# 40 routed units are moved under the last batch's routing, and six batches of the shared network are moved to the end, in an attention and mixture-of-experts block on one core

## The chip, the cores and the metric

The program runs on one core of a Trainium2 chip. The metric is the device time of one execution, in microseconds (us). In the text PE is TensorE (matmuls), DVE is VectorE, ACT is ScalarE, POOL is GpSimd and SP is SyncE, which here only issues DMAs.

## The reference, cut to what matters

The input is 8 batches of 512 tokens with 128 channels. An attention layer with 16 heads runs first, with modulated layer norms around it. Then each token passes a shared network and two of eight routed experts:

```
x = x + ga * attention(norm(x) * (1 + ca) + sa)
h = norm(x) * (1 + cb) + sb
shared   = (silu(h @ shared_gate.T) * (h @ shared_up.T)) @ shared_down.T   # 128 -> 256 -> 128
scores, indices = top_k(sigmoid(h @ router_w.T + routing_bias), 2)         # 2 of 8 experts
w        = scores / sum(scores), spread over the experts
combined = sum over e of w[e] * (silu(h @ gate_w[e]) * (h @ up_w[e])) @ down_w[e]
out = x + gb * (shared + combined)
```

## The kernel before, in words

Every engine has its own program, written out in order; semaphores alone tie the engines together.

**Attention.** A loop over the 8 batches in 16 slots each. In the slots of batch b the kernel also finishes batch b-1: projection, second layer norm, router, ranks within each expert. For every (token, expert) pair a record of 130 floats (the normed token, its weight, the row that its result goes to) is scattered to DRAM (`routed`) by POOL, 8 indirect DMAs of 128 rows a batch (L690). Each expert has a region of its own in `routed`; `next_row` counts how far each region is filled. The scatters of batch b-2 go between POOL's work in the slots of batch b; those of the last two batches come after the loop.

**Shared network.** After the last batch's attention, `shared_up(b, j)` (PE, 4 matmuls of 512 columns, L1590) fills two PSUM banks, `shared_silu(b, j)` (ACT, L901) and `shared_act(b, j)` (DVE, L1162) make the product, `shared_dn(b)` (PE, 16 small matmuls, L1600) projects it back, and `shared_sum(b)` (DVE, L1170 and L1173) multiplies it with the gate `gb` and adds it to `x1`. All eight batches run here, and between them the last batch's projection, norm, router and ranks. When its counts are known, DVE makes tables (`region_tables`, `unit_tables`): which rows each unit reads and which expert it belongs to. SP then writes 128 rows of padding behind the last row of each of the eight regions (L594), one DMA an expert with its row read from a table first.

**Units.** The routed work is cut into 71 units of 128 records of one expert. For unit u SP loads the records (L604), at most 8 units ahead of the last unit that is finished (`yu_ready`); PE transposes them (`unit_T`, L1635); PE multiplies with gate and up (`unit_up`, L1646, 8 passes); ACT takes the silu (L927); DVE multiplies (`unit_act`, L1258); PE multiplies with down (`unit_dn`, L1655); ACT scales with the weight (`unit_y`, L932); POOL scatters the 128 results to DRAM (`send_unit`, L750). DVE also copies each unit's expert weights (L1270) and its result rows (L1253, which waits for the send of unit u-8). In step i PE runs `unit_up(i)`, `unit_T(i + 2)`, `unit_dn(i - 2)`, in that order, and the other engines likewise.

**End.** When all sends have landed, SP and ACT each load one result a batch and token (8 DMAs of 256 KB each, L445), and the sums, the gate and the addition to `x1` follow per batch: on DVE (L1306, L1313, L1316), for every second batch with the first sum on PE. SP and ACT store the output (L450).

Of the kernel before, what the change touches and what calls it, by code (L numbers as in the profile page):

```python
# [44 lines left out]
FAR = 1 << 20  # L45


def adaln_block(nc: bass.Bass, x, Wq, bq, Wk, bk, Wv, bv, Wp, bp, sh_gate, sh_up, sh_down,
                gate_w, up_w, down_w, router_w, routing_bias, c, wmod, out):
    ctx = ExitStack()  # L50
    with ctx:
# [104 lines left out]
        skip = sb("skip", [P, E])  # L156
        entered = sb("entered", [P, UNITS, E])
# [105 lines left out]
        table_chain = sem("table_chain")  # L263
        tables_ready = sem("tables_ready")
# [12 lines left out]
        sums_ready = sem("sums_ready")  # L277
# [76 lines left out]
        def sum_bank(b):  # L354

            return mx_bank[b // 2 % 2][:, 1, :]
# [81 lines left out]
        OUT_ORDER = (0, 2, 1, 4, 3, 6, 5, 7)  # L438

        def move_results(eng, half):  # L440
# [3 lines left out]
            for b in range(B):  # L444
                eng.dma_start(results[b][half], result_v[:, half, b]).then_inc(results_loaded[b], 16)  # L445
            for place, b in enumerate(OUT_ORDER):
                if place % 2 != half:
                    continue
                eng.wait_ge(out_ready, place + 1)
                eng.dma_start(out_v[:, b], x1[:, TT * b:TT * (b + 1), :]).then_inc(out_stored, 16)  # L450
# [5 lines left out]
        def _(sp):  # L456
# [134 lines left out]
            sp.wait_ge(tables_ready, 1)  # L591
            for e in range(E):
                row = sp.value_load(end_row[0:1, e:e + 1], min_val=e * REGION, max_val=e * REGION + TOKENS)
                sp.dma_start(routed_dram[bass.ds(row, P), :], pad_row[:]).then_inc(padding_written, 16)  # L594
            sp.wait_ge(padding_written, 16 * (E + 1))
            sp.wait_ge(scattered, BATCH_ROWS * B)
            sp.wait_ge(tables_ready, 3)
# [8 lines left out]
            for u in range(RING):  # L606
                load_unit(u, u, False)
            for it in range(1, UNITS // RING):
                for slot in range(min(RING, MOST_UNITS - RING * it)):
                    load_unit(RING * it + slot, slot, True)  # L610

            move_results(sp, 0)
# [6 lines left out]
        def _(pool):  # L619
# [87 lines left out]
            def scatter(b):  # L707
# [4 lines left out]
                rows_scattered(b)  # L712
# [30 lines left out]
            rstd(mv2, ve2, var2_ready, rstd2, rstd2_ready, stats2_ready, B_LAST)  # L743
            modulate2(B_LAST)
            scatter(B_LAST)
# [8 lines left out]
            for it in range(0, UNITS // RING):  # L754
                for slot in range(min(RING, MOST_UNITS - RING * it)):
                    send_unit(RING * it + slot, slot)
# [3 lines left out]
        def _(act):  # L760
# [149 lines left out]
            shared_silu(2, 0)  # L910
            shared_silu(2, 1)
            shared_silu(3, 0)
            evacuate_h2T(B_LAST, use(B_LAST, "h2T_last"))
            shared_silu(3, 1)
            exp_minus_logits(B_LAST, use(B_LAST, "lg_last"))
            for b in range(4, B):
                for j in range(IC):
                    shared_silu(b, j)
# [10 lines left out]
            def unit_y(u, slot):  # L929

                act.wait_ge(yu_full, u + 1)
                act.activation(y_u[slot], (pv_bank, misc)[slot % 2][:, 0:C], ACT.Copy, scale=w_u[slot]).then_inc(yu_ready, 1)  # L932

            def unit_step(i, k, turn, has_silu=True, has_xT=True, has_y=True):
                if has_silu:
                    unit_silu(i, k % RING)
                if has_xT:
                    unit_xT(i + 2, (k + 2) % RING)
                if has_y:
                    unit_y(i - 2, (k - 2) % RING)  # L940
# [15 lines left out]
        def _(dve):  # L956
# [207 lines left out]
            def shared_sum(b):  # L1164
# [3 lines left out]
                if b >= 1:  # L1168
                    dve.wait_ge(s_out, b)
# [545 lines left out]
```

## Time and profile before

| | us |
|---|---|
| median of 3 runs (lowest, highest) | 683.39 (681.89, 684.39) |
| the profiled execution, its span | 683.7 |
| attention, to the first matmul of the shared network | 0 to 483.4 |
| shared network, last batch's routing, tables, padding, first loads | 483.4 to 534.7 |
| 71 units, from the first `unit_act` to the last | 534.7 to 656.3 |
| last sends, result loads, final sums, stores | 656.3 to 683.7 |

The page gives one execution. An engine's busy time is the union of its instructions; "idle before" is the time in which it stood, with what ended it behind the arrow. PE's ends are modelled, so that one matmul's length is longer than the distance to the next start.

### The profile page before, as it was taken

The page shows a single profiled execution, that of the slowest core. Times are in us where ns is not written, and L with a number is a line of the kernel's source. Part 1 is how long each engine was busy: PE and PEld are TensorE (multiplying, and loading weights), DVE is VectorE, ACT ScalarE, POOL GpSimd, SP SyncE. Part 2 cuts the span into 40 slices and gives each one's busy share as a digit, 9 for nine tenths or more (in the row PEclk, how much of TensorE's full clock was granted, in tenths as well). Part 3 has the DMA queues.
Part 4 walks back from the last instruction along what each step waited for, and adds up shares of the span by engine and source line. Part 5 has one row for each costly group of instructions (what it writes and reads, how often), then busy time and mean ns, then how long its engine had stood idle before and what let it go on. Part 6 is the DMA issues. An engine that isn't in the chain of part 4 may idle for free.

```text
span 683.7 us, 11593 instructions
## 1 busy us (share of the span) xinstructions
PE 624.5 (91%) x3693; PEld 298.9 (44%) x3693; DVE 516.7 (76%) x1104; ACT 411.0 (60%) x846; POOL 264.0 (39%) x309
## 2 busy tenths in 40 slices
PE   4988999999999999999999999999998898888935
PEld 2332333233333333433333333232465888888931
DVE  5659888889988989888898888983368655555617
ACT  2145777777777687777777777778542445444520
POOL 4221022324352461452434233134434366566540
PEclk9669999999999999999999999999999999999987
DMA  3533132222321233223222231115102222222228
GB/s 101 146 56 97 52 101 76 66 82 72 94 86 62 75 97 95 79 78 105 72 70 75 70 98 52 39 40 173 53 0 70 64 74 78 69 78 79 70 68 320
DMA packets 50064, 56.92 MB, mean 83 GB/s; under 512 B 10281, under 2 KB 39243, under 8 KB 50004
## 3 DMA queue, kind: packets, MB, share of 16 engines
q1 hardware_dynamic: 42648, 43.11, 22.4%
q0 software_dynamic: 4320, 8.47, 3.6%
q10 hardware_dynamic: 3036, 4.61, 2.1%
q8 instruction: 30, 0.49, 0.3%
q14 instruction: 30, 0.25, 0.1%
HBM read 38.36 MB, written 17.92 MB: 82 GB/s over the span
## 4 chain that ended last, share of the span: by engine, by line
PE 68%; DVE 13%; ACT 6%; DMA 4%; issue 4%; SPq 2%; POOL 1%; another core or an unknown queue 0%; ACTq 0%; POOLq 0%; DVEq 0%
PE pv L1457 15%; PE st L1446 14%; PE mx L1431 13%; PE st L1646 9%; DVE neg_max L1012 6%; PE mx L1590 3%; ACT pt L803 2%; PE misc L1324 2%; PE misc L1351 2%; PE pv L1655 2%; PE misc L1655 2%; PE st L1600 1%; PE misc L1357 1%; DMA even_qk<-k_parts 1%; DVE ln L969 1%
## 5 line engine op out<-in xcount | busy, mean ns | idle before, releaser
L803 ACT ACTIVATE pt<-st 128x512 f32<-128x512 f32 x496 | 282.2, 598 | 106.0 <-PE st L1446 96.8
L1012 DVE TENSOR_REDUCE neg_max<-mx 128x2 f32<-128x1024 f32 x248 | 294.4, 1215 | 50.5 <-PE mx L1431 47.3
L1457 PE MATMUL pv<-pt,vs 128*32 128x512 f32 x1024 | 136.4, 605 | 0.3 <-ACT pt L803 0.3
L690 POOL DMA_INDIRECT routed<-rec,row_u x64 | 64.4, 1007 | 142.1 <-PE pv L1457 115.2
L750 POOL DMA_INDIRECT results<-qs,home_u x71 | 77.4, 1091 | 60.5 <-ACT qs L932 42.1
L1446 PE MATMUL st<-even_qk 74*128 74x512 bf16 x256 | 88.9, 388 | 4.1 <-DMA even_qk<-m_rows 2.2
L1446 PE MATMUL st<-qs,ks 74*128 74x512 bf16 x240 | 81.5, 383 | 1.8 <-ACT pt L803 1.1
L1431 PE MATMUL mx<-even_qk 72*128 72x512 bf16 x240 | 74.5, 392 | 6.0 <-DVE neg_max L1012 3.4
L1431 PE MATMUL mx<-ks,qs 72*128 72x512 bf16 x256 | 76.5, 380 | 2.8 <-DVE neg_max L1012 2.5
L1258 DVE TENSOR_TENSOR vs<-vs,st 128x256 f32<-128x256 f32 x71 | 29.7, 418 | 42.6 <-ACT vs L927 31.4
L1646 PE MATMUL st<-vs,pt 128*128 128x128 f32 x376 | 52.0, 282 | 10.3 <-DVE vs L1258 7.4
L398 POOL TENSOR_TENSOR qk_r<-qk_f,qk_parts 128x512 f32<-128x512 f32 x15 | 17.4, 1163 | 108.6 <-DVE qk_parts L390 108.4
L927 ACT ACTIVATE vs<-st 128x256 f32<-128x256 f32 x71 | 27.4, 386 | 45.7 <-PE st L1646 35.1
L1446 PEld LDWEIGHTS st<-even_qk 74*128 74x128 bf16 x256 | 20.7, 98 | 73.2 <-ACT pt L803 51.6
L1646 PEld LDWEIGHTS st<-vs,pt 128*128 128x128 f32 x376 | 46.8, 196 | 12.8 <-ACT vs L922 9.1
L1446 PEld LDWEIGHTS st<-qs,ks 74*128 74x128 bf16 x240 | 18.9, 98 | 67.5 <-ACT pt L803 51.6
L1457 PEld LDWEIGHTS pv<-pt,vs 128*32 128x32 f32 x1024 | 20.1, 108 | 52.9 <-issue 38.1
L1431 PEld LDWEIGHTS mx<-even_qk 72*128 72x128 bf16 x240 | 22.3, 100 | 37.9 <-DVE neg_max L1012 11.6
L1431 PEld LDWEIGHTS mx<-ks,qs 72*128 72x128 bf16 x256 | 23.8, 98 | 31.0 <-DVE neg_max L1012 7.8
L1270 DVE COPY pt<-even_qk 128x768 f32 x47 | 27.6, 588 | 6.2 <-issue 3.1
L1590 PE MATMUL mx<-h2T,shared_w 128*128 128x512 f32 x64 | 29.9, 600 | 1.9 <-issue 1.9
L1646 PE MATMUL st<-vs 128*128 128x128 f32 x192 | 25.9, 278 | 3.7 <-DVE vs L1258 2.5
(199 smaller groups left out, 792.7 us busy)
## 6 DMA issues: line engine op xcount, KB each, us to landing
ks<-routed SPq DMA_DIRECT2D x71, 65.0 KB
even_qk<-q_parts SPq DMA_DIRECT2D x48, 96.0 KB
qs<-q_parts SPq DMA_DIRECT2D x48, 96.0 KB
ks<-k_parts SPq DMA_DIRECT2D x48, 96.0 KB
even_qk<-k_parts SPq DMA_DIRECT2D x42, 96.0 KB
q_parts<-qk_parts SPq DMA_DIRECT2D x21, 128.0 KB
k_parts<-qk_parts SPq DMA_DIRECT2D x7, 384.0 KB, 2.3
x_in<-L_attn_x SPq DMA_DIRECT2D x8, 256.0 KB
```

The source lines that it names most:

```text
L690: pool.indirect_dma_start(out=routed_dram, out_offset=bass.IndirectOffsetOnAxis(ap=row_u[:, k, t:t + 1], axis=0), in_=rec[b.par][:, k, t, ...
L750: pool.indirect_dma_start(out=result_dram, out_offset=bass.IndirectOffsetOnAxis(ap=home_u[:, slot:slot + 1], axis=0), in_=y_u[slot], in_of ...
L803: act.activation(pt[n % 2][:, hh, :], score_bank(b, n, hh), ACT.Exp, scale=SCALE).then_inc(exp_done, 1)
L927: act.activation(silu_u[slot % 2], st_bank[slot % 2][:, 0:I], ACT.Silu).then_inc(silu_ready, 1)
L1012: dve.tensor_reduce(neg_max[g % 2][:, hh, 2 * half:2 * half + 2], mx_bank[half][:], AX_X, ALU.max, negate=True).then_inc(mx_free, 1)
L1258: dve.tensor_tensor(act_u[slot % ARING], silu_u[slot % 2], st_bank[slot % 2][:, I:2 * I], ALU.mult).then_inc(act_ready, 1)
L1270: dve.tensor_copy(w_unit[u % WRING], weights.rearrange("p e i -> p (e i)")[:, bass.ds(first, 3 * I)]).then_inc(w_ready, 1)
L1431: last = pe.matmul(mx_bank[half][:, t, :], qs[b.par][0:PROD, h, q0:q0 + P], ks[b.par][0:PROD, h, :], start=True, stop=True)
L1446: pe.matmul(score_bank(b, n, hh), ks[b.par][0:STACK, h, j * P:(j + 1) * P], qs[b.par][0:STACK, h, :], start=True, stop=True).then_inc(st_f ...
L1457: last = pe.matmul(pv_bank[32 * hh:32 * (hh + 1), :], vs[b.par][:, j, HG * g + hh, :], pt[n % 2][:, hh, :], start=(n % Y_SLOTS == 0), stop ...
L1590: last = pe.matmul(mx_bank[j][:, which, :], shared_w[:, IC * which + j, :], h2T[:, T * b:T * (b + 1)], start=True, stop=True)
L1646: last = pe.matmul(st_bank[slot % 2][:, m * P:(m + 1) * P], w_unit[u % WRING][:, m * P:(m + 1) * P], xuT[slot % 2], start=True, stop=True)
```

## The change

The units are cut into 40 early and 32 late ones. The early units hold only full blocks of 128 records from the first six batches, so they need neither the last two batches' records nor any padding. DVE makes their tables in slots 9 and 10 of the last batch (`early_regions`, `early_units`), and the units start after `shared_sum(0)`. The last batch's transposition, router, choice, ranks and scatters, and the tables of the late units, are interleaved with unit steps 0 to 24. SP writes the padding after the load of unit 31. The shared network of batches 2 to 7 runs after the last unit, and the final sum of a batch takes its result straight from PSUM: DVE adds the two results, adds the shared network's, multiplies with the gate and adds to `x1`. The sums on PE are gone. The order of batches in the end is changed, and SP alone stores the output.

The diff, cut:

```diff
+EARLY = 40
+LATE = UNITS - EARLY
+FIRST_SHARED = 2
+H2T_AT, LOGITS_AT, LIKELIEST_AT, CHOOSE_AT, RANK_AT, SCATTER_AT = 8, 10, 12, 14, 16, 16
+TABLES_AT = 18
...
-        OUT_ORDER = (0, 2, 1, 4, 3, 6, 5, 7)
+        OUT_ORDER = (2, 0, 3, 1, 4, 5, 6, 7)
...
+            sp.wait_ge(early_ready, 1)
+            sp.wait_ge(rows_free, 2 + B - 2)
+            sp.wait_ge(st_full, HG * SLOTS * B)
+            for u in range(MOST_UNITS):
+                if u == EARLY - RING:
+                    pad_regions()
+                if u == EARLY:
+                    sp.wait_ge(padding_written, 16 * (E + 1))
+                    sp.wait_ge(scattered, BATCH_ROWS * B)
+                    sp.wait_ge(tables_ready, 2)
+                load_unit(u, u % RING, u >= RING)
...
             modulate2(B_LAST)
-            scatter(B_LAST)
...
+            for u in range(MOST_UNITS):
+                if u == SCATTER_AT:
+                    hold(pool, rows_ready, B)
+                if SCATTER_AT <= u < SCATTER_AT + K_TOP * TT:
+                    scatter_rows(B_LAST, u - SCATTER_AT)
+                send_unit(u, u % RING)
...
+            for i in range(MOST_UNITS + 2):
+                if i < MOST_UNITS:
+                    unit_silu(i, i % RING)
+                if i + 2 < MOST_UNITS:
+                    unit_xT(i + 2, (i + 2) % RING)
+                if i >= 2:
+                    unit_y(i - 2, (i - 2) % RING)
+                if i == H2T_AT:
+                    evacuate_h2T(B_LAST, use(B_LAST, "h2T_last"))
+                if i == LOGITS_AT + 1:
+                    exp_minus_logits(B_LAST, use(B_LAST, "lg_last"))
+            for b in range(FIRST_SHARED, B):
+                for j in range(IC):
+                    shared_silu(b, j)
+                if b == FIRST_SHARED:
+                    load_results(act, 1)
...
+                    if n == 9 and last:
+                        early_regions()
+                    if n == 10 and last:
+                        early_units()
...
             shared_sum(0)
-            layer_norm2(B_LAST)
-            shared_act(2, 0)
...
+                if i == LIKELIEST_AT:
+                    likeliest(B_LAST)
+                if i == CHOOSE_AT:
+                    choose(B_LAST)
+                if i == RANK_AT:
+                    assign_rows(B_LAST, use(B_LAST, "rank_last"))
+                if i == TABLES_AT:
+                    late_regions()
+                if i == TABLES_AT + 2:
+                    late_entered()
+                if i == TABLES_AT + 4:
+                    late_rows()
+                if i == TABLES_AT + 6:
+                    unit_experts(EARLY, LATE, tables_ready)
...
+            def finish(b):
+                r = results[b][0]
+                add_results(b)
+                dve.wait_ge(s_down, b + 1)
+                dve.tensor_tensor(r, st_bank[b % 2][:].rearrange("p (t c) -> p t c", t=TT), r, ALU.add).then_inc(s_gated, 1)
+                dve.wait_ge(s_gated, b + 1)
+                gate_and_add(b)
...
+            shared_up(2, 0)
+            pe.wait_ge(yu_ready, MOST_UNITS)
+            shared_up(2, 1)
+            for b in range(FIRST_SHARED + 1, B):
+                shared_up(b, 0)
+                shared_dn(b - 1)
+                shared_up(b, 1)
             shared_dn(B - 1)
```

Three places show what the change does to the order on the engines. The first is SP at the load of unit 31 and the two loads behind it, in the changed kernel; `L594` and `L598` there are the load of a unit, `L604` and `L605` the padding.

```order
L594 TENSOR_LOAD unit_row
L594 ISA x2
L598 ISA
L598 DMA ks<-routed 128x130
L604 TENSOR_LOAD end_row
L604 ISA x2
L605 ISA
L605 DMA routed<-pad_row 128x130
L604 TENSOR_LOAD end_row
```

The group of the last five rows stands there eight times, and the load of unit 32 comes behind them; before, the eight stood ahead of the load of unit 0.

The second is DVE between the multiplications of units 11 and 14 of the changed kernel (`L1281` is `unit_act`, `L1276` the copy of the result rows, `L1293` the copy of the expert's weights, `L1060` to `L1065` is `likeliest`).

```order
L1281 TENSOR_TENSOR vs<-vs,st 128x256
L1276 CAST home_u<-ks 128x1
L1060 TENSOR_SCALAR probs<-probs 128x32
L1061 RECIPROCAL probs<-probs 128x32
L1063 MAX top_p<-probs 128x8 x4
L1065 MAX_INDEX top_e<-top_p,probs 128x8 x4
L1290 REGISTER_ALU x2
L1290 ISA
L1293 ISA
L1293 COPY pt<-even_qk 128x768
L1281 TENSOR_TENSOR vs<-vs,st 128x256
```

Before, `likeliest` stood directly ahead of `choose` and the shared products, and no unit was under way.

The third is ACT at the end. Before, it stood so (`L932` is `unit_y`, `L445` a result load, `L450` a store):

```order
L932 ACTIVATE qs<-pv,ks 128x128
L445 DMA qs<-results 128x512 x4
L445 DMA ks<-results 128x512 x4
L450 DMA out<-x 128x512 x4
```

In the changed kernel it stands so (`L913` is `shared_silu`, `L451` a result load):

```order
L935 ACTIVATE qs<-pv,ks 128x128
L913 ACTIVATE pt<-mx 128x512 x2
L451 DMA qs<-results 128x512 x4
L451 DMA ks<-results 128x512 x4
L913 ACTIVATE pt<-mx 128x512 x10
```

Ten of the twelve silus of the shared network now stand behind the eight result loads on ACT.

## Rows read from the trace of the kernel before

**Rows 1.** Busy us of PE, PEld, DVE, ACT, POOL; clock; DMA share, GB/s, by stage.

```profile
483.40:534.68 51.28, 48.09 (x244) 31.27 (x241) 35.53 (x100) 17.01 (x28) 21.93 (x23) 1.00 0.14 39
534.68:656.31 121.63, 107.86 (x905) 103.87 (x904) 69.62 (x208) 58.34 (x206) 73.09 (x67) 0.99 0.26 72
656.31:683.70 27.39, 10.41 (x24) 4.13 (x23) 13.71 (x21) 1.10 (x3) 4.34 (x5) 0.77 0.65 232
```

**Rows 2.** The chain of waits in the shared network: start, us, what.

```profile
490.85 1.72 PE mx L1590 x4
492.57 1.78 PE st L1600 x16
```

**Rows 3.** Timeline of DVE (start, us, engine, line), from the shared network to unit 0.

```profile
495.36 0.69 DVE L1170 TENSOR_TENSOR pt<-st,gb_bc 128x512 f32<-128x512 f32 x1 [1.43 <-PE st L1600]
...
529.86 1.03 DVE L1270 COPY vs<-even_qk 128x768 f32 x2 [0.59 <-issue]
...
534.68 0.41 DVE L1258 TENSOR_TENSOR vs<-vs,st 128x256 f32<-128x256 f32 x1
```

**Rows 4.** Timeline of PE, two unit steps in a row.

```profile
599.10 1.06 PE L1646 MATMUL st<-vs,pt 128*128 128x128 f32 x8
...
600.54 1.06 PE L1646 MATMUL st<-vs,pt 128*128 128x128 f32 x8
```

**Rows 5.** DVE in stretches: length, busy us and count, clock, DMA share, GB/s.

```profile
476.00:477.72 1.72, 1.56 (x14) 1.00 1.16 330
477.70:478.85 1.15, 0.98 (x7) 1.00 1.18 288
482.10:483.05 0.95, 0.84 (x5) 1.00 0.00 0
513.65:515.24 1.59, 1.41 (x8) 1.00 0.01 5
521.90:524.68 2.78, 2.64 (x7) 1.00 0.34 103
```

**Rows 6.** Timeline of DVE, late in the last batch.

```profile
471.81 0.36 DVE L1028 RECIPROCAL y_rden<-misc 128x32 f32<-128x32 f32 x1 [5.03 <-PE misc L1324]
```

**Rows 7.** Timeline of PE, the last batch's router.

```profile
505.07 0.96 PE L1393 MATMUL misc<-router_T,h2T_now 128*128 128x8 f32 x8
```

**Rows 8.** Timeline of ACT, behind the last batch's exponential.

```profile
506.54 1.28 ACT L901 ACT_TABLE_LOAD   x1
507.88 0.60 ACT L901 ACTIVATE pt<-mx 128x512 f32<-128x512 f32 x1
```

**Rows 9.** Timeline: padding writes, first two loads, first transposition, load 40 and its transposition.

```profile
514.87 10.68 SPq L594 DMA_DIRECT2D routed<-pad_row  x8
...
527.53 1.49 SPq L604 DMA_DIRECT2D ks<-routed  x2
...
529.62 0.30 PE L1635 MATMUL mx<-ident,ks 128*128 128x128 f32 x1
...
593.53 0.45 SPq L604 DMA_DIRECT2D ks<-routed  x1
...
598.54 0.27 PE L1635 MATMUL mx<-ident,ks 128*128 128x128 f32 x1
```

**Rows 10.** Timeline of PE, a unit's matmuls after a pause.

```profile
633.86 2.05 PE L1646 MATMUL st<-vs,pt 128*128 128x128 f32 x8 [2.69 <-DVE vs L1258]
```

**Rows 11.** The stretch after it, columns as in rows 1.

```profile
634.00:636.00 2.00, 2.00 (x10) 2.00 (x11) 1.20 (x4) 0.44 (x3) 1.15 (x2) 0.50 0.16 36
```

**Rows 12.** Timeline of the end: last send, ACT's later four loads, last DVE additions.

```profile
660.88 0.98 POOL L750 DMA_INDIRECT results<-qs,home_u  x1 [0.30 <-issue]
...
664.98 2.30 ACTq L445 DMA_DIRECT2D ks<-results  x4
...
679.26 0.69 DVE L1316 TENSOR_TENSOR x<-x,ks 128x512 f32<-128x512 f32 x1
...
680.58 0.69 DVE L1316 TENSOR_TENSOR x<-x,ks 128x512 f32<-128x512 f32 x1
```

More of the change, by code:

```diff
@@ new lines, in _ @@
+            for i in range(MOST_UNITS):
+                ahead = i + 2
+                if ahead < MOST_UNITS:
+                    if ahead == EARLY:
+                        dve.wait_ge(tables_ready, 3)
+                    if ahead % RING == 0:
+                        experts = [experts_of(ahead // RING)]
+                    unit_weights(ahead, ahead % RING, experts[0], ahead >= WRING)
+                unit_act(i, i % RING)
+                if ahead < MOST_UNITS:
+                    unit_rows(ahead, ahead % RING, ahead // RING, ahead >= RING)
+                if i == 0:
+                    layer_norm2(B_LAST)
+                if i == LOGITS_AT:
+                    add_router_bias(B_LAST, use(B_LAST, "lg_last"))
+                if i == LIKELIEST_AT:
[12 more added lines that the diff above has]
+                    unit_experts(EARLY, LATE, tables_ready)
@@ L1319, in _ @@
+            shared_act(3, 0)
+            finish(2)
+            shared_act(3, 1)
+            shared_act(4, 0)
+            finish_first(0)
+            finish(3)
+            shared_act(4, 1)
+            shared_act(5, 0)
+            finish_first(1)
+            finish(4)
+            shared_act(5, 1)
+            shared_act(6, 0)
+            finish(5)
+            shared_act(6, 1)
+            shared_act(7, 0)
+            finish(6)
+            shared_act(7, 1)
+            finish(7)
         @block.tensor
@@ L1680, in _ @@
-            for i in range(UNITS - RING, MOST_UNITS + 2):
-                unit_step(i, i - UNITS + RING, UNITS // RING - 1, has_up=i < MOST_UNITS, has_T=i + 2 < MOST_UNITS)
-            for b in range(1, B, 2):
-                pe.wait_ge(results_loaded[b], 16 * K_TOP)
-                if b >= 4:
-                    before = OUT_ORDER[:OUT_ORDER.index(b - 4) + 1]
-                    pe.wait_ge(out_chain, sum(2 - k % 2 for k in before))
-                for k in range(K_TOP):
-                    last = pe.matmul(sum_bank(b), ident[:], results[b][k].rearrange("p t c -> p (t c)"),
-                                     start=(k == 0), stop=(k == K_TOP - 1))
-                last.then_inc(sums_ready, 1)
+            shared_dn(1)
@@ new lines, in _ @@
+            pe.wait_ge(routed_loaded, 64)
+            for i in range(MOST_UNITS + 2):
+                if i < 2:
+                    pe.wait_ge(s_gated, FIRST_SHARED - 1 + i)
+                if i < MOST_UNITS:
+                    unit_up(i, i % RING, i >= 2)
+                if i + 2 < MOST_UNITS:
+                    unit_T(i + 2, (i + 2) % RING, (i + 2) // RING)
+                if i >= 2:
+                    unit_dn(i - 2, (i - 2) % RING, i >= 4)
+                if i == H2T_AT:
+                    h2_T(B_LAST, use(B_LAST, "h2T_last"))
+                if i == LOGITS_AT:
+                    router_logits(use(B_LAST, "lg_last"))
+                if i == RANK_AT:
+                    ranks(B_LAST, use(B_LAST, "rank_last"))
```

276 lines of the change are left out of this document (99 added, 177 removed).

## The prediction

> **What bounds the kernel now.** I first cut the span into stages and read each one's busy times. From 483.4 to 534.7 us PE is busy 48.1 of 51.3 us; in the units 107.9 of 121.6 us; in the end it is nearly idle, and the DMA engines are busy two thirds of 27.4 us [rows 1]. The reader is to see that PE, the bound of two stages, stands by in the third. I then read single steps there. A unit step takes PE 1.44 us [rows 4], but 71 units take 121.6, or 1.74 each: about a sixth goes into waits that come and go. A batch of the shared network costs PE two groups of 1.72 and one of 1.78 [rows 2], 5.2 us; six batches are 31.3 us. Moved into the end, they would seem to cost nothing. So I priced three things: how much earlier unit 0 starts, what the units lose by what is put between them, and how much longer the end becomes. All times below go against this execution's 683.7 us; the median of the runs shown is 683.4.
>
> **Earlier start.** After `shared_sum(0)`, whose first operation stands at 495.36 [rows 3] and which is two operations of some 0.7 us, DVE goes on at once with the units: 0.59 us for the table value and 1.03 for two copies of weights [rows 3] to 498.4, `shared_sum(1)` 1.4, two row copies 0.2, a third weight copy 0.5, so the first `unit_act` stands at 500.5 instead of 534.68 [rows 3]. PE is ready by then: its transpositions and `shared_dn(1)` end at about 497. The loads can't be late: SP issues them during the shared network's first two batches, and the experts' weights, in flight at 478.8, have landed at 482.1, when the DMA engines are idle [rows 5]. The early tables are some 21 small operations, 5.5 us at the 0.2 us of their like (1.59 for 8, rows 5 fourth) and a little more for the wide ones; DVE stands 5.03 us in that place [rows 6], so I count 0.5 lost. Without that cover they would cost up to 5.5 on PE's way to the last scores. Gain: 34.2 - 0.5 = 33.7; bounds 32 and 34.5.
>
> **What is put between the units.** PE gets the transposition, router and ranks; the router is 0.96 [rows 7], all three some 1.4 us, and PE is the bound, so 1.4 is the lower bound for the whole part. For the other engines I use what a step leaves over: DVE is busy 69.6 us for 71 units [rows 1], 0.98 each, and has register instructions between, so about 0.3 of a step is spare, and with two PSUM banks a product may come about 1 us late before it holds `unit_up` two units on. So a block alone costs its length less 1.0, and one that follows two steps later its length less 0.6:
> - `likeliest` 1.7 [rows 5]: 0.7. `choose` 1.15 [rows 5]: 0.2, its marks aren't urgent. `assign_rows` waits for the ranks, which PE makes behind `unit_dn`, about 1.3, and takes 0.95 [rows 5]: 1.2.
> - late tables: `late_regions` one operation more than the 1.59 [rows 5]: 0.8. `late_entered` 1.4: 0.8. `late_rows` is five operations of the row of 2.78 for seven [rows 5], over 32 units instead of 72, so 1.55: 0.9. `unit_experts` 0.7: 0.1.
> - layer norm and the wait for the router's sums: 0.9.
> - the exponential on ACT: two table loads and 0.23. A load is 1.28 and the next function starts 1.34 after it began [rows 8], so 2.9, and silu, `unit_xT` and `unit_y` stand behind it: 1.9.
>
> Together with PE's 1.4: 8.9. The upper bound is all lengths in full, 18. For the table load I weighed a page of the Trainium skill, "ScalarE: Activation LUTs", section "What ACT_TABLE_LOAD costs": each switch is 1.28 us and as much again for draining, 2.66 in all. By that, the sum would be 2.6 higher; the row shows the silu 0.06 us behind the load's end, so I keep the row.
>
> **The padding.** Before, SP's eight padding writes took 10.68 us from issue to issue [rows 9] while nothing waited but the first load. Now they stand between the loads of units 31 and 32, and all later loads are queued behind them. Two loads back to back take 1.49 us from the first issue to the end of the second, of 0.37 or so [rows 9], so a load costs SP 1.12 us, and a write has the same instructions. At that rate SP is 9.0 us busy with the eight, at their measured rate 10.7. Load 32 is thus 8.4 to 10.1 us later than in a row of loads 1.74 apart. What it has to spare is load 40's distance to its transposition, 598.54 - 593.53 = 5.0, less the shortest, 529.62 - 527.53 = 2.1 [rows 9]: 2.9. So PE stands 5.5 to 7.2 us at `unit_T(32)`, and with it `unit_dn(30)`. I take 5.5: POOL's eight scatters fall into the same time and hold the loads back a little anyway. A pause of this length brings the low clock: after one of 2.69 us eight passes took 2.05 instead of 1.06 [rows 4, 10], at a granted clock of 0.50 [rows 11]. I count 1.7 for it: the 0.99 of the eight passes and as much of the step's rest. Part: 7.2; bounds 3 (mostly hidden) and 9.
>
> **The end.** T is the last `unit_act`. The last send starts at T + 4.57, and ACT's loads end at 667.28, T + 11.0 [rows 12]. In the changed kernel ACT has done the two silus of batch 2 by then, but the other ten stand behind the loads, so DVE gets the product (3, 0) at T + 11.6. From there it has 10 products, six batches with four operations and two with three: 40 operations. Two of them, one waiting for the other, take 1.32 [rows 12], so 40 take 26.4. PE isn't done in time everywhere. Up to product (5, 1) DVE has first-batch results to fill in and waits once, 0.9, so that stands at T + 28.1. From then on a batch is a circle: `shared_dn` some 0.6 behind the product (it loads it as weights, an estimate), 1.78, `shared_up` 1.72, silu 0.8, product 0.65, that is 5.6, twice, then 2.6 for the last `shared_dn` and 2.0 for three operations: T + 44.0. The last store needs the 2.4 that it needs now (681.27 to 683.7). End T + 46.5 instead of T + 27.4: 19.1 longer. The result loads themselves are hidden by then. If ACT's queue didn't hold the silus, 2 us less; with PE at half clock for a part, more.
>
> **Sum.** 683.7 - 33.7 + 8.9 + 7.2 + 19.1 = 685.2. I forecast 685.2, no difference that counts: 0.5% (3.4 us) is about what a measurement of this kernel can tell.
>
> **Rivals.**
> - *The padding is hidden* (faster): if the eight writes leave load 32 within its 2.9 us, or if the late tables' steps stretch so that it has more to spare, 7.2 falls away, and half of the 8.9 goes into waits that are there anyway (the sixth of the stage in rows 1 against rows 4): 674 to 679. For it: single waits of 2 us stand in the units already [rows 10]. Against it: 9 us are three times what there is to spare. It decides at about 5 us less. Chance 0.28.
> - *POOL's scatters hold the units* (slower): one is 0.98 + 0.30 [rows 12], a pair of scatter and send 2.56 against a step of 1.74, so after eight units POOL is 6.5 behind. DVE's row copy of unit u waits for the send of u - 8, with some 4 us to spare. If this stall comes before the padding's and not in it, 2 to 4 more, and the upper half of the DVE bounds with it: 688 to 693. Chance 0.2.
> - *PE loses the clock in the end* (slower): in my schedule PE stands 1.8 and 2.2 us about T + 12 and T + 16 and is busy three quarters of the rest. At 1.2 GHz over some 10 us the end grows by 4.4, over all of it by 18: 690 to 703. Against it: in the units it is busy 89% at a clock of 0.99, waits included [rows 1]. "TensorE: Matmul & The Clock Gate" of the Trainium skill, section "A second HAM failure mode: psum-queue depth-cycling", says that PE can swing between its clocks when it idles briefly and often between groups; no row of these shows that. Chance 0.16.
> - The forecast, 680.0 to 686.8, keeps 0.36.
>
> **Range and chances.** 675 to 695 leaves out the best of the first rival and most of the clock's. Faster by over 0.5% 0.28, within 0.36, slower 0.36. The forecast's own range is 681 to 690, from the bounds of the padding and the end.
>
> **What would show it.** First `unit_act` at 500 to 501; units from there to the last in about 137.7 us (121.6 + 16.1); one stop of PE of over 4 us at unit 32, with SP's queue full of padding writes, and a clock of 0.50 behind it; ACT's eight loads ahead of its third silu in the end and DVE idle some 5 us there; the end 46 us long, DVE busy about 28 of them. The prediction is wrong if the stop isn't there, if the steps 8 to 24 aren't slower than the others, or if the end is shorter than 42.

## The result, and the profile after

The changed kernel takes 702.78 us (median of 4 runs, 693.68 to 703.91) where the kernel before took 682.64 on the same chip: ratio 1.025 (1.0185 to 1.032). The forecast was 685.2, the range ended at 695. It is slower, and outside the range. One of the four runs, at 693.68, lies inside it. The profiles below are read by their spans, which are about 1.7 us shorter than these times: 700.6 for the changed kernel, 683.7 before, from which the forecast was worked out.

The stages of the changed kernel, columns as in [rows 1]: last maxima to first shared product, to unit 0's `unit_act`, to that of unit 24, of 40, of 70, to the end.

```profile
469.69:495.07 25.38, 21.04 (x126) 5.74 (x124) 14.31 (x55) 18.20 (x36) 7.20 (x9) 0.93 0.45 133
495.07:513.90 18.83, 16.67 (x88) 12.12 (x84) 9.57 (x25) 5.85 (x11) 9.07 (x10) 0.91 0.22 55
513.90:565.05 51.15, 38.94 (x319) 36.48 (x318) 33.30 (x123) 24.04 (x76) 32.03 (x32) 0.98 0.22 61
565.05:602.03 36.98, 29.43 (x221) 28.73 (x220) 17.15 (x52) 13.67 (x47) 20.43 (x20) 0.89 0.31 82
602.03:653.50 51.47, 44.98 (x379) 43.12 (x379) 29.45 (x87) 25.70 (x90) 31.20 (x29) 1.00 0.25 69
653.50:700.60 47.10, 35.96 (x148) 21.51 (x148) 28.37 (x43) 7.91 (x15) 3.89 (x4) 0.92 0.38 134
```

In the kernel before, the same six stages took 20.75, 51.30, 40.90, 29.14, 51.59 and 27.39 us. The reader is to see that the units (139.6 us, forecast 137.7) and the end (47.1, forecast 46.5) are nearly as forecast, and that unit 0 is not: it starts at 513.90, forecast was 500.5 and 0.5 for the early tables. From 500.5 it is 13.4 us, which stand in three places.

**7.1 us lie ahead of everything that the change touches.** The last batch's last maxima stand at 469.69 instead of 462.62. One stretch of the setup, first of the kernel before, then of the changed one:

```profile
24.00:64.80 40.80, 35.21 (x119) 12.01 (x118) 26.50 (x36) 16.39 (x29) 7.58 (x11) 0.72 0.46 113
```

```profile
24.00:64.80 40.80, 33.66 (x86) 11.18 (x86) 21.74 (x31) 11.53 (x20) 7.84 (x11) 0.50 0.37 91
```

The granted clock is 0.50 throughout; in the kernel before it is 1.0 for good from 50.1 us. PE is nearly as busy (33.66 us and 35.21) and does 86 operations instead of 119. The instructions there are the same.

**4.6 us are the early tables** (25.38 against 20.75; I had counted 0.5). The timeline of DVE, some of the 21 operations:

```profile
473.95 0.17 DVE L1154 TENSOR_SCALAR padded_i<-padded 128x8 int32<-128x8 f32 x1
474.16 1.13 DVE L1121 TENSOR_SCALAR padded_i<-padded_i 128x8 int32<-128x8 int32 x1
475.32 1.19 DVE L1122 CAST padded<-padded_i 128x8 f32<-128x8 int32 x1
476.55 0.22 DVE L1123 TENSOR_TENSOR entered<-earlier,padded 128x64 f32<-128x64 f32 x1
...
477.98 1.19 DVE L1158 TENSOR_TENSOR taken<-taken,padded 128x8 f32<-128x8 f32 x1
...
482.66 0.35 DVE L1031 RECIPROCAL y_rden<-misc 128x32 f32<-128x32 f32 x1
```

What POOL did beside them:

```profile
472.63 1.27 POOL L686 TENSOR_TENSOR ln<-ln,mod_now 128x512 f32<-128x512 f32 x1 [1.79 <-POOLq L706]
473.98 2.51 POOL L691 TENSOR_TENSOR rec<-ln,mod_now 128x512 f32<-128x512 f32 x2
...
477.88 1.26 POOL L680 TENSOR_TENSOR x_ep<-x_ep,bp_ga 128x512 f32<-128x512 f32 x1
```

Three operations of eight elements a row take 1.1 to 1.2 us, six times the 0.17 of their like, and they end where POOL's 1.26 us products do (the last two at 476.5 and 479.1). The chain of 21 takes 9.0 us from 473.77, the reciprocal stands 12.97 us behind the maxima (9.19 before, [rows 6]), and PE waits for what follows it. The kernel before has the same products of POOL in the very stretch in which its DVE stood idle, 466.78 to 471.81:

```profile
466.66 2.51 POOL L681 TENSOR_TENSOR rec<-ln,mod_now 128x512 f32<-128x512 f32 x2
...
470.57 1.26 POOL L670 TENSOR_TENSOR x_ep<-x_ep,bp_ga 128x512 f32<-128x512 f32 x1
```

PE in the changed kernel, columns as in [rows 10], and the stretch behind its stop:

```profile
483.58 1.06 PE L1463 MATMUL misc<-router_T,h2T_now 128*128 128x8 f32 x8 [2.55 <-DVE y_tok L1034]
484.50 0.83 PE L1516 MATMUL mx<-qs,ks 74*128 74x512 bf16 x2
485.26 1.94 PE L1527 MATMUL pv<-pt,vs 128*32 128x512 f32 x8
...
488.57 1.07 PE L1527 MATMUL pv<-pt,vs 128*32 128x512 f32 x8
```

```profile
484.72:488.13 3.41, 3.41 (x13) 0.64 (x12) 1.94 (x17) 1.56 (x4) 0.00 (x0) 0.50 0.72 179
```

Behind the stop of 2.55 us the granted clock is 0.50 for 3.4 us, and the products take 1.94 instead of 1.07. **The remaining 1.7 us** are in the two shared batches (18.83 against a forecast of 17.1). They go with the chip: this stage takes 15.89 to 15.90 us in seven profiles on the faster chips of the experiments, and 18.8 to 19.2 in eight on the slower ones, this one among them.

The padding stop came where it was forecast, at unit 32: SP's queue, then PE. It is 4.0 us long (forecast 5.5; 4.75 and 4.90 in two later profiles).

```profile
570.73 9.11 SPq L605 DMA_DIRECT2D routed<-pad_row  x8
580.60 9.72 SPq L598 DMA_DIRECT2D ks<-routed  x8
```

```profile
582.64 0.33 PE L1689 MATMUL mx<-ident,ks 128*128 128x128 f32 x1 [4.03 <-DMA ks<-routed]
...
585.63 1.77 PE L1700 MATMUL st<-vs,pt 128*128 128x128 f32 x8
```

ACT's loads in the end came as forecast too: its third silu stands 6.44 us behind the second.

```profile
658.16 0.60 ACT L913 ACTIVATE pt<-mx 128x512 f32<-128x512 f32 x1 [1.12 <-issue]
661.25 1.80 ACTq L451 DMA_DIRECT2D qs<-results  x4
663.08 2.08 ACTq L451 DMA_DIRECT2D ks<-results  x4
665.20 1.08 ACT L913 ACTIVATE pt<-mx 128x512 f32<-128x512 f32 x2 [6.44 <-issue]
```

### The profile page after: what moved, and what is told of

It reads as the page before. It is cut to its first block, busy times and chain, and to the rows that moved or that the text cites. A ratio compares the mean times of both kernels' runs of the same rounds, so it can differ in the third digit from the quotient of the medians.

```text
span 700.6 us, 11557 instructions
## 1 busy us (share of the span) xinstructions
PE 631.8 (90%) x3677; PEld 302.4 (43%) x3677; DVE 524.0 (75%) x1126; ACT 412.0 (59%) x846; POOL 261.6 (37%) x309
## 4 chain that ended last, share of the span: by engine, by line
PE 63%; DVE 14%; issue 7%; ACT 6%; DMA 4%; SPq 2%; another core or an unknown queue 1%; POOL 1%; ACTq 1%; DVEq 0%; POOLq 0%
PE pv L1527 15%; PE st L1516 15%; PE mx L1501 14%; PE st L1700 5%; DVE neg_max L1015 5%; PE misc L1421 2%; PE misc L1394 2%; PE mx L1660 2%; PE st L1670 2%; ACT pt L815 2%; DMA even_qk<-k_parts 1%; PE pv L1709 1%; PE misc L1427 1%; DVE ln L972 1%
## 5 line engine op out<-in xcount | busy, mean ns | idle before, releaser
L1527 PE MATMUL pv<-pt,vs 128*32 128x512 f32 x1024 | 139.0, 615 | 0.3 <-ACT pt L815 0.3
L759 POOL DMA_INDIRECT results<-qs,home_u x71 | 73.9, 1041 | 52.6 <-ACT qs L935 31.5
L1516 PE MATMUL st<-even_qk 74*128 74x512 bf16 x256 | 90.4, 394 | 3.1 <-DMA even_qk<-m_rows 1.2
L1501 PE MATMUL mx<-even_qk 72*128 72x512 bf16 x240 | 77.3, 405 | 8.9 <-DMA even_qk<-k_parts 6.0
L1281 DVE TENSOR_TENSOR vs<-vs,st 128x256 f32<-128x256 f32 x71 | 29.7, 418 | 46.9 <-ACT vs L930 29.7
L1293 DVE COPY pt<-even_qk 128x768 f32 x47 | 28.2, 600 | 6.3 <-issue 4.2
L913 ACT ACTIVATE pt<-mx 128x512 f32<-128x512 f32 x16 | 9.4, 597 | 38.2 <-PE mx L1660 23.4
```

Of the source, the lines that this page charges most:

```text
L759: pool.indirect_dma_start(out=result_dram, out_offset=bass.IndirectOffsetOnAxis(ap=home_u[:, slot:slot + 1], axis=0), in_=y_u[slot], in_of ...
L1281: dve.tensor_tensor(act_u[slot % ARING], silu_u[slot % 2], st_bank[slot % 2][:, I:2 * I], ALU.mult).then_inc(act_ready, 1)
L1293: dve.tensor_copy(w_unit[u % WRING], weights.rearrange("p e i -> p (e i)")[:, bass.ds(first, 3 * I)]).then_inc(w_ready, 1)
L1501: last = pe.matmul(mx_bank[half][:, t, :], qs[b.par][0:PROD, h, q0:q0 + P], ks[b.par][0:PROD, h, :], start=True, stop=True)
L1516: pe.matmul(score_bank(b, n, hh), ks[b.par][0:STACK, h, j * P:(j + 1) * P], qs[b.par][0:STACK, h, :], start=True, stop=True).then_inc(st_f ...
L1527: last = pe.matmul(pv_bank[32 * hh:32 * (hh + 1), :], vs[b.par][:, j, HG * g + hh, :], pt[n % 2][:, hh, :], start=(n % Y_SLOTS == 0), stop ...
```

## Experiments

The runs were made in four sets, on chips of two kinds: on some the kernel before takes 665 us, on others, as on the first, 683 to 688. Each run is compared with the kernel before on its own chip.

**1. Both kernels again** (nothing edited; 665.27 us before).

> The changed kernel once more, to see how its first 66 us vary. In the profile of the change the code up to 66 us is the same as before, yet DVE's operations there stand 7.0 us later from 59 us on, and the granted clock stayed at 0.5 from 23.9 to 64.9 us instead of returning at 39.8 and for good at 50.1. Theory A (the setup can go two ways in any execution, whatever stands later in the program): the runs fall into two groups some 7 to 10 us apart, 692 to 694 and 701 to 704, and the unchanged kernel has both groups too. Theory B (the change brings it, by where its code or data lie): nearly all runs stand at 701 to 704, and the unchanged kernel's stay at 681 to 684.

> The kernel before once more, beside it. Theory A: some of its runs stand 7 to 10 us above the others, at 689 to 692. Theory B: all of them stand at 681 to 685, and the clock in its profile returns for good near 50 us.

Measured: changed 677.11, ratio 1.0155 (1.0112 to 1.0199); before 665.36. The long stretch of low clock was there again, from 23.0 to 64.0 us, and the last maxima stood 3.4 us later than in the kernel before. Neither theory came out whole. Four of the changed kernel's six runs stand at 676.8 to 679.4 and two at 669.5 and 672.9, while all 35 of the kernel before stand between 661.6 and 672.7, without a second group: this speaks against A, and the two lower runs against B. The kernel was run once more, in the set of experiment 3:

> The changed kernel, nothing altered. Two of its two profiled executions had the lower clock from 23 to 64 us, four of four of the others had it only to 41 to 53 us. Theory (the setup, whose code the change doesn't touch, falls into the longer lower clock by chance in any kernel): its times split into two groups 3 to 4 us apart, and the profile may show either. Rival (this program falls into it nearly always): 677 us, 0.5 to 64 us in the profile again.

Measured: 673.18 (670.39 to 685.55), ratio 1.0133; this time the clock was back at 51.1 us, so the program doesn't fall into the long stretch every time. The stages of this profile, and behind them those of the kernel before on the chip of the first set:

```profile
462.97:488.28 25.31, 20.98 (x127) 5.69 (x125) 14.23 (x55) 18.09 (x36) 7.18 (x9) 0.93 0.45 133
488.28:504.17 15.89, 15.07 (x88) 10.54 (x84) 9.47 (x25) 5.96 (x11) 9.07 (x10) 1.00 0.26 64
504.17:547.63 43.46, 37.41 (x320) 36.04 (x320) 33.11 (x124) 25.24 (x76) 30.41 (x29) 1.00 0.25 70
547.63:579.36 31.73, 25.77 (x209) 25.26 (x208) 18.11 (x52) 14.31 (x47) 21.30 (x22) 0.89 0.33 93
579.36:622.73 43.37, 43.37 (x391) 43.37 (x391) 30.26 (x88) 27.39 (x89) 32.05 (x30) 1.00 0.29 83
622.73:668.64 45.91, 35.17 (x152) 20.58 (x151) 28.34 (x43) 8.16 (x15) 4.46 (x5) 0.96 0.38 139
```

```profile
465.32:486.08 20.76, 19.16 (x127) 5.66 (x125) 6.19 (x34) 18.00 (x36) 7.21 (x9) 1.00 0.54 159
486.08:536.98 50.90, 47.99 (x244) 31.28 (x241) 35.77 (x99) 16.90 (x28) 22.21 (x23) 1.00 0.14 40
536.98:571.18 34.20, 34.20 (x309) 34.20 (x308) 24.08 (x74) 21.37 (x71) 23.88 (x22) 1.00 0.30 84
571.18:594.49 23.31, 23.31 (x212) 23.31 (x210) 16.93 (x49) 14.85 (x49) 17.42 (x17) 1.00 0.33 92
594.49:637.58 43.09, 43.09 (x389) 43.09 (x388) 29.57 (x89) 27.14 (x88) 32.05 (x31) 1.00 0.31 85
637.58:664.66 27.08, 11.18 (x24) 4.32 (x23) 13.71 (x21) 1.10 (x3) 3.84 (x4) 0.79 0.65 235
```

Here the sum can be read without the setup: -35.0 + 4.6 (start), +9.3 (steps 0 to 24), +8.4 (24 to 40), +0.3, +18.8 (end) make +6.3 us (before rounding); forecast was +1.5. The first profile has the same differences stage by stage to 1 us, but for its 7.1 us in the setup and 2.5 in the shared batches.

**2. Each suspected cost mended alone** (the same set as 1). The early tables go into the slot of `choose`, behind the router's softmax:

```diff
-                    if n == 9 and last:
+                    if n == 14 and last:
                         early_regions()
-                    if n == 10 and last:
                         early_units()
```

> The changed kernel with the early tables made in slot 14 of the last batch, behind the choice, instead of in slots 9 and 10. In the change's profile the tables took DVE 8.8 us (473.8 to 482.7) where it had 5.0 free, the router's matmuls waited 2.55 us for it, the clock fell to 0.5 for 3.4 us, and the first shared matmul stood 4.6 us later against the last batch's slot 9. Theory (tables on PE's way): the first shared matmul comes 4 to 5 us earlier measured from slot 9, the time falls by 4 to 5 against the changed kernel. Rival (ACT's exponentials bound the last slots and take it back, or the tables now delay the ranks of batch 6 and with them POOL): less than 1.5 us.

Measured: 668.12, ratio 1.0037 (1.0005 to 1.0068), 9.0 less than unmended. Two of the long operations, now beside an idle POOL, in DVE's timeline:

```profile
482.11 0.17 DVE L1121 TENSOR_SCALAR padded_i<-padded_i 128x8 int32<-128x8 int32 x1
482.32 0.17 DVE L1122 CAST padded<-padded_i 128x8 f32<-128x8 int32 x1
```

All 21 now take 5.5 us. The last maxima to the first shared product take 20.75 us again: 4.6 of the 9.0. Another 3.1 is that this profile's setup had its clock back at 52.7 us; the rest is not assigned.

The padding goes out as one write ahead of each load of units 29 to 36:

```diff
-                if u == EARLY - RING:
-                    pad_regions()
+                if u == PAD_FROM:
+                    sp.wait_ge(tables_ready, 1)
+                if PAD_FROM <= u < PAD_FROM + E:
+                    pad_region(u - PAD_FROM)
```

> The changed kernel with one padding write ahead of each of the loads of units 29 to 36, instead of all eight ahead of the load of unit 32. In the change's profile PE stood 4.0 us for the transposition of unit 32, with the clock at 0.5 behind it. Theory (the eight writes in a row hold the loads longer than they have to spare): no stop of PE over 2 us at units 29 to 37, and 4 to 6 us less. Rival (SP is short of time over the whole stretch: 2.3 us a load against a step of 1.5 to 1.7): the stop is only spread, 0 to 2 us less.

Measured: 671.69, ratio 1.0100 (1.0075 to 1.0125). Steps 24 to 40 go from 31.5 to 27.3 us, 4.2 back of the 8.4; the stop at unit 32 is gone. The tables, still in slots 9 and 10, cost more here: low clock for 17 us goes with their stop, and the stage took 31.25 us.

```profile
474.57:491.63 17.06, 17.06 (x67) 4.12 (x67) 3.56 (x27) 7.40 (x15) 0.00 (x0) 0.50 0.25 64
```

**3. Both mended, the scatters spread, the setup kept busy** (665.1 us before).

> Both mendings in one kernel: the early tables in slot 14, and one padding write ahead of each load of units 29 to 36. Theory (two separate costs of the change, 9.0 us for the early tables in slots 9 and 10 and 4.2 us for the padding's eight writes in a row): the two add, so some 664 us where the kernel before takes 665.3 and the unchanged changed kernel 677.1, ratio 0.998; last maxima to first shared product 20.75 us, steps 24 to 40 in 27.3 us. Rival (the tables' gain was mostly a good state of the setup, which came by chance): the ratio stays at 1.004 or above, near that of the tables alone, whatever the padding gives.

Measured: 663.97, ratio 0.998 (0.9957 to 1.0004). The rival as it was put (1.004 or more) is out, and the two costs add, but not as 9.0 and 4.2. Beside the unmended kernel of its own set (673.18) the gain is 9.2 us, and the stages hold 4.6 for the tables and 4.6 for the padding; the 9.0 of experiment 2 had some 3 us of the setup's chance in it, as the rival suspected. Steps 24 to 40 take 27.2 us, still 3.9 more than before. POOL's queue has no pause from 530.85 to 569.00 us:

```profile
530.85:569.00 38.15, 32.43 (x280) 31.46 (x279) 26.20 (x88) 19.88 (x66) 29.61 (x29) 1.00 0.37 101
```

These are 29 transfers, most of them 1.28 us apart (busy 0.96 to 1.4, then 0.30 of issue), and DVE waits 7.7 us in five waits of units 0 to 40 for result sends to land (5.6 of them in steps 24 to 40); in the unmended kernel it was 9.6 in six, in the kernel before none. PE waits for no load there. So I spread the scatters:

```diff
-                if SCATTER_AT <= u < SCATTER_AT + K_TOP * TT:
-                    scatter_rows(B_LAST, u - SCATTER_AT)
+                if SCATTER_AT <= u < SCATTER_AT + 2 * K_TOP * TT and (u - SCATTER_AT) % 2 == 0:
+                    scatter_rows(B_LAST, (u - SCATTER_AT) // 2)
```

> The kernel of both mendings, with the last batch's eight scatters on GpSimd's queue ahead of every second send (units 16, 18 ... 30) instead of ahead of eight sends in a row (16 to 23). In the run with the padding spread, steps 24 to 40 still took 27.3 us, 4.0 more than in the kernel before, and VectorE waited there 2.94, 0.94 and 1.22 us for the result sends. Theory (GpSimd at 1.28 us an indirect transfer falls behind in units 16 to 23, at two transfers for a unit of 1.45 us): these waits shrink to 1 us or less in all, steps 24 to 40 take 24 to 25 us, and the time falls by 2 to 4 us against the kernel of both mendings. Rival (the sends are late for another reason, or GpSimd, 40 of 55 us busy, only falls behind later): steps 24 to 40 stay at 27 us, or the wait moves to load 40, which needs the last scatter: 0 to 1 us gained.

Measured: 662.63, ratio 0.9969 (0.9943 to 0.9995); steps 24 to 40 still 27.1 us. The theory's waits shrank there (from 5.6 us, the longest 3.0, to 4.1, the longest 1.0), but the time of the stage did not: PE now waits 2.8 us in four waits for SP's loads, which stand between the padding writes (a load and a write 2.2 us together, a unit step 1.45). Shortening one wait brought up the next, much as the rival had it.

The setup gets four more products ahead of the wait for the first keys.

```diff
+                if fill == DIRECT_FILLS:
+                    for _ in range(4):
+                        pe.matmul(pv_bank[:], ident[:], direct[1][0][:], start=True, stop=True)
                 max_scores(*fill_of(fill))
```

> The changed kernel, with four more products of 128x128 by 128x512 in TensorE's queue at the place in the setup where it waits for the first keys (2.3 to 6.0 us idle); their result is never read. Theory (the setup's 3 to 7 us come from the lower clock behind that idle stretch): the clock is at 1.0 for good by 53 us or sooner, the last maxima come 3 us sooner than in the changed kernel, and the median is 3 us lower. Rival (the idle stretch has nothing to do with it, or the late keys set the times themselves): lower clock to 64 us and the same time, or up to 4 us more where the products stand in the way.

Measured: 675.85, ratio 1.0161, no gain. Its profile had the clock back for good at 51.1 us, but so had the unedited run beside it: this settles nothing. Its early tables were followed by 13.7 us of low clock, and that stage took 29.63 us.

**4. GpSimd's queue, the loads, the modulation.** The first three of these fell on a chip where the kernel before takes 687.12 us, without the kernel of both mendings beside them; so a second set (687.66 before) repeated two of them with it.

```diff
                     scatter_rows(B_LAST, u - SCATTER_AT)
+                    if u % 2 == 1:
+                        scatter_rows(B_LAST, u - SCATTER_AT, spare_dram)
```

> The kernel of both mendings, with four more indirect transfers on GpSimd's queue (behind the scatters of units 17, 19, 21 and 23; the same rows into a spare buffer that nobody reads). In the kernel of both mendings GpSimd runs without a pause from 531 to 569 us, at 1.28 us a transfer, while units 16 to 40 are worked on. Theory (with the padding spread, GpSimd's queue is what the units wait for there: 24 sends and 8 scatters at 1.28 us are 41 us, and 24 units alone would be 35): steps 24 to 40 take 27.2 + 4 x 1.28 = 32.3 us, and the time rises by 5 us to 669. Rival (GpSimd is busy but nobody waits for it; steps 24 to 40 are long for the padding writes that still stand between the loads): no more than 1 us.

> The kernel of both mendings again, as the yardstick for the three others of this set: the runs with more scatters, with the loads by SyncE and with the modulation on VectorE fell on a chip where units 0 to 70 take 20 us more in every kernel (the kernel before included) and no run of the kernel of both mendings stood beside them. Theory (the mendings leave the changed kernel level with the one before): ratio 0.995 to 1.002 where the kernel before takes 665 us, and some 1.005 where it takes 685.

> The four more indirect transfers on GpSimd's queue again, now beside the same kernel without them. Theory (GpSimd's queue is what units 24 to 40 wait for once the padding is spread): 5.1 us above the kernel of both mendings, all of it in steps 16 to 40. Rival: within 1 us of it.

Measured: 698.35 (first set); 692.93 with the mendings alone (ratio 1.0085, 1.0043 to 1.0127) and 698.92 with four more transfers (1.0172, 1.0122 to 1.0222): 6.0 us (give or take 4.5, an estimate from the two intervals) for 5.1 us of GpSimd's time. In the first set the next run below, whose units are those of both mendings, serves as the yardstick: 692.61, or 5.7 less. So more transfers cost time, and of the size expected. The mechanism isn't shown. In the profiles of the second set the stretch from unit 0 to 24 takes 62.6 instead of 55.2 us and 24 to 40 takes 32.4 instead of 30.6; in the first set it is 59.7 and 58.7, then 34.7 and 31.9. And the wait that the theory goes by, DVE for a result send, is 1.2 us in all in either kernel of the second set. The mended kernel itself is level with the one before at 665 us and 0.85% slower here.

All result loads by SyncE:

```diff
-            load_results(sp, 0)
+            load_results(sp)
...
-                if b == FIRST_SHARED:
-                    load_results(act, 1)
```

> The kernel of both mendings, with all sixteen loads of results issued by SyncE, none by ScalarE. The prediction's step: ScalarE's eight loads hold its queue behind the last unit, and the third batch's silus with it, for 1.8 us, with VectorE idle for some 5 us there. Theory (the step as predicted): the end, from the last unit_act, goes from 46.8 us to 45, and the time falls by 1 to 2 us to 662 or 663. Rival (the sixteen loads on one queue come later than the sums want them, or the end is bound by the results' sends): no gain, or up to 2 us lost.

Measured: 692.61, ratio 1.0088 (1.0056 to 1.012), against 1.0085 for the mendings alone in the other set: no gain to be seen in the time, though the end is 43.2 us in this profile and 44.4 in the other. In DVE's timeline the third product no longer waits for ACT's queue, and the first addition waits for its load instead:

```profile
653.83 0.69 DVE L1248 TENSOR_TENSOR pt<-pt,mx 128x512 f32<-128x512 f32 x1 [1.03 <-ACT pt L915]
657.03 0.69 DVE L1344 TENSOR_TENSOR qs<-qs 128x512 f32<-128x512 f32 x1 [2.51 <-DMA qs<-results]
```

The last batch's modulation on VectorE, at units 1 to 3:

```diff
+                if i == 1:
+                    dve.wait_ge(ln2_ready, TT * B)
+                    dve.tensor_tensor(ln2[:], ln2[:], mod_now[B_LAST.par][:, 2:3, :].to_broadcast([P, TT, C]),
+                                      ALU.mult).then_inc(h2_chain, 1)
+                if i in (2, 3):
...
+                    dve.tensor_tensor(rec[B_LAST.par][:, i - 2, :, 0:C], ln2[:],
+                                      mod_now[B_LAST.par][:, 1:2, :].to_broadcast([P, TT, C]), ALU.add).then_inc(h2_ready, 1)
```

> The kernel of both mendings, with the last batch's three modulation products (1.52, 1.51 and 1.51 us on GpSimd, at units 1 to 3) made by VectorE, ahead of its work for units 2 to 4. Theory (two engines that read and write the same memory hold each other up: VectorE's weight copies of 1.23 us at units 3 to 5, 0.55 elsewhere, and the small operations of 1.2 us in the early tables, are as long as they are because a GpSimd product runs beside them; and the first send waits behind these products): the copies take 0.56 us each, VectorE's wait of 2.0 us for the sends at unit 8 goes, VectorE pays 3 x 0.7 = 2.1 us, and steps 0 to 24 come out 1 to 3 us shorter, 40.5 to 42.5 us. Rival (the long copies have another cause, such as TensorE's or the transfers' use of the memory): the copies stay at 1.23 us and steps 0 to 24 grow by some 2 us.

> The last batch's modulation products on VectorE again, beside the same kernel with them on GpSimd. The first run showed every weight copy at 0.55 us (1.23 where GpSimd's products ran beside them) and steps 1 to 4 at 1.46 us (1.55). Theory: steps 0 to 24 are 1 to 3 us shorter and the time falls by as much. Rival (what is won at the copies is paid for by the products on VectorE, and the backlog of GpSimd at units 16 to 40 eats the earlier start): the same time within 1 us.

Measured: 690.79 (ratio 1.0053) and 691.92 (1.0063; 1.0 less than the mendings alone in its set, which is within the scatter). Weight copies in DVE's timeline, of the kernel of both mendings, then of this one:

```profile
505.76 0.56 DVE L1293 COPY pt<-even_qk 128x768 f32 x1
506.65 1.22 DVE L1293 COPY pt<-even_qk 128x768 f32 x1
508.18 1.23 DVE L1293 COPY pt<-even_qk 128x768 f32 x1
```

```profile
505.34 0.56 DVE L1296 COPY pt<-even_qk 128x768 f32 x1
506.80 0.56 DVE L1296 COPY pt<-even_qk 128x768 f32 x1
508.27 0.56 DVE L1296 COPY pt<-even_qk 128x768 f32 x1
```

Without POOL's products the long copies are gone: that part of the theory is shown. Steps 0 to 24 are 51.9 us instead of 55.2, DVE's own products included, but 24 to 40 are 32.7 instead of 30.6. Most of the gain is given back there, as the rival had it.

**5. All of it in one kernel.**

> All mendings in one kernel: early tables in slot 14, one padding write per load, scatters ahead of every second send, all loads of results by SyncE, the last batch's modulation on VectorE. Theory (each gain stands by itself: 1.3 us for the scatters, 1 to 2 for the loads, 1 to 3 for the modulation, from 664): 658 to 661 us where the kernel before takes 665, ratio 0.990 to 0.994. Rival (they share one limit, GpSimd's 48 transfers from unit 0 to unit 40, and the gains don't add): 662 to 663, ratio 0.996.

Measured: 687.60, ratio 1.0012 (0.9979 to 1.0046), 5.3 us less than both mendings alone. Against the kernel before it is a draw: both the expected 0.990 to 0.994 and the rival's 0.996 were missed. Two parts of it had gained 1.3 and 1.0 us, the third none that showed, each within its own scatter, so I can't say which carries the 5.3.

## Why the prediction was wrong

By spans the forecast was missed by 15.4 us: 7.1 in the setup, 4.1 at the early tables, 1.7 in the two shared batches, 1.3 between the units, 0.6 at the padding, 0.6 in the end.

- *Earlier start.* The 34.2 us were nearly right: 35.0 on the faster chips and 32.5 on the first, without the setup and the tables. **The step of the sum that failed is "I count 0.5 lost" for the early tables.** Their length, 5.5 us, was right for a place where POOL makes no product: in slot 14 they measured just that. Their cover was taken from [rows 6], which doesn't show what POOL does meanwhile. Three operations wait out a POOL product each: 9.0 us in 5.0 us of cover. The reciprocal comes 3.8 us late for it; the other 0.8 go with the low clock behind PE's stop. It is 4.6 us in three profiles of the changed kernel, 8.9 and 10.5 in two edits that left the tables there. Moving them removes all of it. The prediction named the right bound ("without that cover up to 5.5 on PE's way") and ruled it out; nothing in it priced low clock there.
- *A term that the sum didn't have.* **The largest part of the miss was put at nothing:** the sum starts from the span before and lets the attention stand as it was. Against the kernel before on the same chip, 7.1 us (first chip) and 3.4 (second) stand in the setup, in profiles whose clock stays low to 64 us. Two of three profiles of the changed kernel have it, none of thirteen of the kernel before and of edits that leave the setup alone. The edits that don't have it differ from the changed kernel only behind it, and its own third profile hasn't it, so the change's work isn't the cause. Whether chance or how the program lies in memory makes it frequent stays open, and so does its exact size: the last maxima of the profiles without it stand anywhere from 460.6 to 465.6. It was no case of the range. Without it the time would have been about 695.7 (estimate, 702.8 less 7.1), at the range's edge; whether the forecast fell outside was thus a matter of luck too, but the 4.1 us of the tables were not.
- *Between the units.* 8.9 forecast, 10.2, 9.6 and 9.3 measured in the three profiles. The size is right, part of the mechanism isn't: I charged DVE's blocks and ACT's table loads, but on the faster chips DVE waits 9.6 and 9.0 us for result sends up to unit 40, which start late behind POOL's modulation, and the copies beside that modulation are 0.67 longer. In the first profile the wait for sends is named for only 0.7 us, and the longest part of DVE's waiting there is for ACT's silu (17.0).
- *The padding.* 7.2 forecast; steps 24 to 40 grew by 7.8, 8.2 and 8.4. The stop, its place and the clock of 0.50 are there. But spreading the writes gives back only 4.2 to 4.6, so the eight writes in a row cost less than the term, and that the stage came out near it is luck. What makes the other 3.9 isn't shown. The rival of the scatters, given 0.2 as an alternative, names a wait that is there on the faster chips (DVE for the send of u - 8, 5.6 us in these steps); when it shrank to 4.1 in experiment 3 the steps grew no shorter, since SP's loads came next.
- *The end.* 19.1 forecast, 19.7, 20.5 and 18.8 measured. The circle of 5.6 us a batch (the last four `shared_dn` are 6.3, 5.3 and 5.1 us apart in the first profile) and ACT's held silus are as drawn. That the held silus cost 2 us is not borne out: with SyncE's loads DVE waits for the load instead, the end is 1.2 us shorter in the profile, and the time is not.
- *The other rivals.* The clock in the end was 0.91 to 0.96, and the end grew by no more than 1.4 us over the forecast. The padding wasn't hidden: the stop is there.

## What to carry to other kernels

Before small operations are put into an engine's idle stretch, look at the timelines of both engines that share the memory there, not at the idle time of one. When a stage nearly fills one queue, count all its transfers against the stage's length, and then do the same for the next queue: here reordering the transfers of one shortened its waits, and the waits for another took their place. Work moved under transfers is not free because its engine stands idle there: here 31 us of TensorE's time became a chain of sums, products and loads, 5.6 us a batch, and gave back more than half of what the earlier start won. And a forecast for one chip doesn't hold to a per cent on another: run the kernel before beside every edit.

## What the runs showed of the hardware that was not expected

- VectorE's operations stand still beside GpSimd's products on the same memory: 128x8 operations take 1.13 to 1.22 us instead of 0.17, weight copies of 128x768 1.23 instead of 0.56. The extra is 0.7 to 1.1 us here, less than one GpSimd product (1.26). It is always three operations of the chain in five profiles, but not always the same three.
- With the stop of TensorE at the early tables went 3.4 us of low clock in three profiles of the changed kernel and 13.7 and 17.1 us in two edits of it, with the same instructions around it.
- The same program takes 683 to 688 us on some chips and 665 on others, the kernel before too. In the kernel before, the whole difference lies in the units: steps 0 to 70 take 121.6 us on the first and 100.6 on the second, with steps 1 to 3 us longer every five or six units on the first. In the changed kernel the two shared batches are 3 us longer there too. What makes these waits isn't settled: the trace puts most of ACT's down to TensorE's products, which take no longer there, and they last up to 2.7 us where they last up to 0.9 on the second. One wait of VectorE in the shared batches, in the kernel of both mendings, first on a chip of the faster kind, then on one of the slower:

```profile
494.44 0.69 DVE L1257 TENSOR_TENSOR pt<-st,gb_bc 128x512 f32<-128x512 f32 x1 [0.47 <-PE st L1670]
```

```profile
499.48 0.69 DVE L1257 TENSOR_TENSOR pt<-st,gb_bc 128x512 f32<-128x512 f32 x1 [3.61 <-PE st L1670]
```
